# A graph network's first layer regrouped by source, and edge weights spread by a matmul

## The reference

```python
x = ln(x + segment_sum(x[src], dst))                      # first layer
x = ln(x + passes(x))                                     # ten passes
x = ln(x + convolutions(x))                               # three gated graph convolutions
x = ln(x + mean_by_dst(mlp([x[dst], x[src] - x[dst]])))   # last stage

def one_pass(f):                                          # ten times
    up = maximum(f[dst] - f[src], 0) * sqrt(w)[:, None]
    return f + maximum(segment_max(up, src), 0)
def gcn(x, W, b):                                         # with self loops and both degrees' roots
    return segment_sum(nw[:, None] * (x @ W)[src], dst) + b
```

## Time and profile before

| | |
|---|---|
| median of 3 runs | 9774.35 us (9773.21 to 9776.04) |
| the profiled execution | 9777.86 us, its span 9776.1 |
| mean granted clock of PE | 0.922 |
| busy: PE, DVE, ACT, POOL | 7043.3, 7381.2, 4251.3, 3651.6 us |
| DMA | 1233.58 MB, mean 126 GB/s |
| first matmul of the passes | 2521.5 us |
| one pass | 440 us, of which 58 steps take 401 |
| one convolution layer | 554.6 us |

### The profile page before, as it was taken

The page is one execution under the profiler, slowest core; times in us unless marked ns, Lnnn a source line. Parts: engine busy times, 40 slices in busy tenths (PEclk is TensorE's granted clock), DMA queues, the critical chain, the costliest instruction groups (busy, mean ns, idle before and its releaser), DMA issues. The chain is left out here.

```text
span 9776.1 us, 146679 instructions
## 1 busy us (share of the span) xinstructions
PE 7043.3 (72%) x44075; PEld 3621.5 (37%) x44075; DVE 7381.2 (76%) x11812; ACT 4251.3 (43%) x4937; POOL 3651.6 (37%) x3081
## 2 busy tenths in 40 slices
PE   3101299990688797979788797979698988946665
PEld 2101255550333343434343343434354555523332
DVE  8877788872687787878787787878798998954443
ACT  0000066660455454545455454545354545523333
POOL 0047788882233332423333332424100000057775
PEclk9999999995899999999999999999799999977777
DMA  2000011115776676767676676767311112111111
GB/s 83 3 11 5 6 37 42 39 37 194 241 234 216 203 243 206 242 206 241 205 233 213 206 245 206 242 204 245 90 61 51 61 46 65 63 16 27 27 27 26
DMA packets 593297, 1233.58 MB, mean 126 GB/s; under 512 B 128487, under 2 KB 241975, under 8 KB 592418
## 3 DMA queue, kind: packets, MB, share of 16 engines
q1 hardware_dynamic: 263170, 851.76, 27.2%
q10 hardware_dynamic: 231360, 335.60, 9.4%
q0 software_dynamic: 97984, 36.11, 3.1%
HBM read 992.41 MB, written 231.17 MB: 125 GB/s over the span
## 5 line engine op out<-in xcount | busy, mean ns | idle before, releaser
L1449 PE MATMUL acc<-dst_hot,parts 128*128 128x512 bf16 x11600 | 2983.3, 382 | 904.5 <-issue 665.2
L1508 ACT ACTIVATE parts_out<-acc 96x1024 bf16<-96x1024 f32 x2320 | 2314.2, 1018 | 2273.7 <-PE acc L1460 1764.0
L1413 POOL DMA_INDIRECT group_best<-best_dram,best_row x1250 | 1469.5, 1176 | 3148.4 <-SPq L1379 2773.4
L1338 DVE TENSOR_SCALAR dst_hot<-dst_rows,node_f 128x2048 bf16<-128x2048 int16 x2910 | 2047.3, 738 | 172.9 <-PE acc L1460 141.1
L1449 PEld LDWEIGHTS acc<-dst_hot,parts 128*128 x11600 | 1047.3, 97 | 2202.6 <-issue 945.5
L907 POOL DMA_INDIRECT gathered<-table_dram,gather_index x830 | 961.1, 1158 | 1967.2 <-POOLq L156 1706.8
L298 POOL DMA_INDIRECT got_src<-edges_dram,gather_index x928 | 1165.4, 1256 | 849.9 <-DVEq L746 558.8
L1460 PE MATMUL acc<-source,parts 128*128 128x128 bf16 x9280 | 909.4, 221 | 3.4 <-issue 0.3
L1006 PE MATMUL acc<-hot_space,parts 128*96 128x512 bf16 x3828 | 857.8, 380 | 42.7 <-DVE hot_space L931 42.5
L1826 DVE TENSOR_SCALAR dst_hots<-node_row,dst_col 128x640 bf16<-128x640 int16 x2436 | 827.4, 382 | 54.7
L1531 DVE SCALAR_TENSOR_TENSOR risen<-rise,factor 128x512 f32<-128x512 f32 x580 | 400.9, 691 | 606.9 <-DMA joined<-slot_inside_dram 459.6
(11 more groups left out here) (369 smaller groups left out, 7999.6 us busy)
## 6 DMA issues: line engine op xcount, KB each, us to landing
dst_rows<-step_dst_dram SPq DMA_DIRECT2D x582, 512.0 KB, 4.5
source<-source_dram SPq DMA_DIRECT2D x582, 512.0 KB, 7.8
best_dram<-best_out ACTq DMA_DIRECT2D x580, 256.0 KB
factor<-slot_weight_dram ACTq DMA_DIRECT2D x560, 256.0 KB
sources<-source_dram SPq DMA_DIRECT2D x174, 512.0 KB, 3.3
joined<-slot_inside_dram ACTq DMA_DIRECT2D x560, 64.0 KB
dst_rows<-step_src_dram SPq DMA_DIRECT2D x58, 512.0 KB, 5.9
source_dram<-source SPq DMA_DIRECT2D x58, 512.0 KB, 6.8
```

The lines of the kernel that those rows point to most:

```text
L1338: nc.vector.tensor_scalar(hot[k % 2][b][:, :], index_rows[k % 3][:, :], node_f[:, b:b + 1], None, ALU.is_equal).then_inc(hot_ready, 1)
L1413: pool.indirect_dma_start(group_best[:, g, h, :], None, best_dram, bass.IndirectOffsetOnAxis(ap=best_row[:, i:i + 1], axis=0)).then_inc(en ...
L1449: nc.tensor.matmul(acc[n % 3][:, 0:TILE], blocks[b], hot[k % 2][b][:, q * TILE:(q + 1) * TILE], start=(b == 0), stop=(b == DST_BLOCKS - 1))
L1508: act.activation(moved[n % (2 * QUADS)][:, :], acc[n % 3][0:SPLIT, :], ACT.Copy).then_inc(tile_moved, 1)
```

## The change

The first layer works on the slots by source: 58 steps as in a convolution layer, 16 source finds and 16 adds on PE with one-hots of 640 columns (all 16 by DVE), sums of all nodes in PSUM. DVE makes the source one-hots of each step in the same loop and SP stores them. The records of 20 steps (320 gathers) are fetched in the preparation, by an index turned to columns from the sorted keys with 16 transposes on PE, and the other 608 in this layer, each into its own column of `got`. After the loop the sums are closed, copied, transposed and added (25 matmuls), normalised and split; dst and root of the weight are turned to rows, the root split in three bfloat16 parts, and both stored by step. The old first layer and the separate source stage go, with the DRAM copies of dst, root and weight.

In the passes `joined` is resident, loaded once in the prologue (128 x 58 x 512 bytes). The weights come as 12 rows of 512 (three DMAs of four rows on SP's queue, after the source load and before the index load of a step); PE multiplies them with a 96 x 128 matrix `spread` after quad 1, before sum_up, and ACT copies the result to `factor` after quad 2's move. There are two PSUM pairs `acc` in place of three.

In the convolutions dst and weight columns are resident, so their preparation only normalises and stores the root; the two casts are made by ACT at quads 2 and 3, the last subtraction moves to stage 7, and PE's address arithmetic stands between the adds. In the last stage `inside` is built after hot_columns(0).

```diff
-RECORDS_FIRST = 400
+STEPS_FIRST = 20
+
+def gather_records(pool, k, got_in):
+
+    for n in range(k * STEP_SUBS, (k + 1) * STEP_SUBS):
+        pool.indirect_dma_start(got[:, n, :], None, edges_dram,
+                                bass.IndirectOffsetOnAxis(ap=record_index[:, n:n + 1], axis=0)).then_inc(got_in, 16)
...
+            for q in range(QUADS):
+                sp.dma_start(key_rows[:, q, :], sorted_dram[0, q * STEPS1 * TILE:(q + 1) * STEPS1 * TILE].rearrange("(k s) -> k s", k=STEPS1)).then_inc(key_rows_in, 16)
...
+                dve.wait_ge(key_cols_moved, 2)
+                link(V.tensor_scalar(record_index[:, :], col_key[:, :].bitcast(U32), ID_MASK, None, ALU.bitwise_and))
                 V.drain().then_inc(edge_ready, 1)
+                key_of(col_key[:, :], col_key[:, :])
+                group_of(group_base[:, :], col_key[:, :])
+                link(V.tensor_scalar(group_base[:, :], group_base[:, :], float(DST_NODES), None, ALU.mult))
+                dve.wait_ge(keys_in0, 16 * (4 + QUADS - 1))
...
-            link(V.memset(inside[1][:, :, :, 0:1], 0))
-            link(V.tensor_scalar(tmp[:, :], starts[1][:, :], -1.0, 1.0, ALU.mult, ALU.add))
-            for k in range(CHUNKS):
-                link(V.tensor_copy(inside[1][:, k, :, 1:CT + 1], tmp[:, k * CT:(k + 1) * CT].unsqueeze(1).broadcast_to([P, D, CT])))
...
+        def _(pool):
+            pool.iota(node_row[:, :], [[1, DST_NODES]], base=0, channel_multiplier=0).then_inc(const_done, 1)
+            for k in range(STEPS_FIRST, STEPS1):
+                if k >= STEPS_FIRST + 4:
+                    pool.wait_ge(got_in[k % 4], records_of(k - 4))
+                gather_records(pool, k, got_in[k % 4])
+            for k in range(STEPS1 - 4, STEPS1):
+                pool.wait_ge(got_in[k % 4], records_of(k))
...
+            for k in range(STEPS1 + 1):
+                if k < STEPS1:
+                    if k >= 2:
+                        sp.wait_ge(source_ready, k - 1)
+                    sp.dma_start(index_rows[k % 2][:, :], step_row(step_src_dram, k)).then_inc(src_in[k % 2], 16)
+                if k:
+                    c = k - 1
+                    sp.wait_ge(source_ready, c + 1)
+                    sp.dma_start(source_dram[c], source[c % 3][:, :]).then_inc(made_out[c % 3], 16)
...
+
+            def columns_of(some):
+                link(V.scalar_tensor_tensor(dst_col[:, some], got[:, some, 0], 1.0, group_base[:, some], ALU.mult, ALU.subtract))
+            columns_of(slice(0, STEPS_FIRST * STEP_SUBS))
+            for k in range(STEPS1 + 1):
+                if k < STEPS1:
+                    dve.wait_ge(src_in[k % 2], 16 * (k // 2 + 1))
+                    if k >= 3:
+                        dve.wait_ge(made_out[k % 3], 16 * (k // 3))
+                        dve.wait_ge(tile_found, (k - 2) * QUADS)
+                    V.tensor_scalar(source[k % 3][:, :], index_rows[k % 2][:, :], node_f[:, 0:1], None, ALU.is_equal).then_inc(source_ready, 1)
+                c = k - 1
+                if c >= STEPS_FIRST:
+                    dve.wait_ge(got_in[c % 4], records_of(c))
+                    columns_of(slice(c * STEP_SUBS, (c + 1) * STEP_SUBS))
+                for n in range(c * STEP_SUBS, (c + 1) * STEP_SUBS) if c >= 0 else ():
+                    if n >= HOTS1:
+                        dve.wait_ge(added, n - HOTS1 + 1)
+                    V.tensor_scalar(dst_hot[n % HOTS1][:, :], node_row[:, :], dst_col[:, n:n + 1], None, ALU.is_equal).then_inc(hot_ready, 1)
...
+            turn_columns(dst_col).then_inc(dst_turned, 1)
+            for h in range(HI):
+                b, at = divmod(h, BANK // D)
+                last = nc.tensor.matmul(sums[:, b * BANK + at * D:b * BANK + (at + 1) * D], flat_first[:, h * P:(h + 1) * P], sum_f[:, :], start=True, stop=True)
+            last.then_inc(rows_done, 1)
+            turn_columns(root_col).then_inc(weight_turned, 1)
...
+            for g in range(DST_GROUPS):
+                V.tensor_copy(flat_first[:, g * DST_NODES:g * DST_NODES + BANK], sums[0:SPLIT, g * BANK:(g + 1) * BANK])
+            V.drain().then_inc(flat_ready, 1)
+            dve.wait_ge(root_done, 1)
+            link(V.tensor_tensor(root_col[:, :], root_col[:, :], is_real[:, :], ALU.mult))
+            V.drain().then_inc(weight_ready, 1)
+            dve.wait_ge(rows_moved, 1)
+            layer_norm(dve, link, norm_ready, norm_root, 1, state[:, :, :], ends[:, :, :])
+            link(V.tensor_copy(rows[:, :, :], state[:, :, :]))
+            split_rows(link, rows[:, :, :])
+            dve.wait_ge(weight_moved, 1)
+            for i in range(3):
+                link(V.tensor_copy(root_parts[:, i, :], root_rows[:, :]))
+                if i < 2:
+                    link(V.tensor_tensor(root_rows[:, :], root_rows[:, :], root_parts[:, i, :], ALU.subtract))
+            V.drain().then_inc(weight_split, 1)
...
     def load_factor(sp, k, factor_in):
-        sp.dma_start(factor[k % 3][:, :], quads_of(slot_weight_dram, k).unsqueeze(1).broadcast_to([QUADS, D, TILE])).then_inc(factor_in[k % 3], 16)
-        sp.dma_start(joined[k % 3][:, :], quads_of(slot_inside_dram, k).unsqueeze(1).broadcast_to([QUADS, D, TILE])).then_inc(factor_in[k % 3], 16)
+        for i in range(3):
+            sp.dma_start(weight_rows[k % 3][i * D:i * D + QUADS, :], step_weight_dram[k, i]).then_inc(factor_in[k % 3], 16)
...
+            for q in range(QUADS):
+                of_quad = slot_inside_dram[q * STEPS1 * TILE:(q + 1) * STEPS1 * TILE]
+                sp.dma_start(joined[q * D:(q + 1) * D, :, :].rearrange("p k s -> p (k s)"), of_quad.partition_broadcast(D)).then_inc(joined_in, 16)
...
+                    if AHEAD <= k + 1 < STEPS1:
+                        if k >= 2:
+                            sp.wait_ge(factor_done, k - 1)
+                        load_factor(sp, k + 1, factor_in)
...
-                    if n >= 3:
-                        pe.wait_ge(tile_moved, n - 2)
+                    if n >= ACCS:
+                        pe.wait_ge(tile_moved, n - ACCS + 1)
...
+                def spread_weights(k):
+                    if k >= AHEAD:
+                        pe.wait_ge(factor_in[k % 3], 48 * loads_before(k))
+                    if k >= 2:
+                        pe.wait_ge(factor_moved, k - 1)
+                    nc.tensor.matmul(factor_sum[k % 2][:, :], spread[:, :], weight_rows[k % 3][:, :], start=True, stop=True).then_inc(factor_done, 1)
...
-                        if q == 1 and k:
-                            sum_up(k - 1)
+                        if q == 1:
+                            spread_weights(k)
+                            if k:
+                                sum_up(k - 1)
...
-                    if q == 2 and 2 <= k + 1 < STEPS1:
-                        if k >= 2:
-                            act.wait_ge(best_ready, k - 1)
-                        load_factor(act, k + 1, factor_in)
                     if q == 3 and k >= 2:
                         store_best(k - 2)
                     act.wait_ge(tile_done, n + 1)
                     if n >= 2 * QUADS:
                         act.wait_ge(sum_done, n // QUADS - 1)
-                    act.activation(moved[n % (2 * QUADS)][:, :], acc[n % 3][0:SPLIT, :], ACT.Copy).then_inc(tile_moved, 1)
+                    act.activation(moved[n % (2 * QUADS)][:, :], acc[n % ACCS][0:SPLIT, :], ACT.Copy).then_inc(tile_moved, 1)
+                    if q == 2:
+                        if k >= 2:
+                            act.wait_ge(risen_ready, k - 1)
+                        act.wait_ge(factor_done, k + 1)
+                        act.activation(factor[k % 2][:, :], factor_sum[k % 2][:, :], ACT.Copy).then_inc(factor_moved, 1)
...
-                    if c >= AHEAD:
-                        dve.wait_ge(factor_in[c % 3], 32 * loads_before(c))
-                    V.scalar_tensor_tensor(risen[:, :], rise[c % 2][:, :], 0.0, factor[c % 3][:, :], ALU.max, ALU.mult).then_inc(risen_ready, 1)
+                    dve.wait_ge(factor_moved, c + 1)
+                    V.scalar_tensor_tensor(risen[:, :], rise[c % 2][:, :], 0.0, factor[c % 2][:, :], ALU.max, ALU.mult).then_inc(risen_ready, 1)
...
+                def cast(c, i):
+                    if not 0 <= c < STEPS1:
+                        return
+                    act.wait_ge(weighed_ready, 2 * c + i + 1)
+                    if not i and c >= 2:
+                        act.wait_ge(added, (c - 1) * STEP_SUBS)
+                    act.activation(message[c % 2][:, :, i * D:(i + 1) * D], weighed[c % 2][:, :, :], ACT.Copy).then_inc(part_ready, 1)
...
+                    if q == 2:
+                        cast(k - 1, 0)
+                    if q == 3:
+                        cast(k - 1, 1)
...
-                        of_step = w_col[:, :].rearrange("p (q k j) -> p k q j", q=QUADS, j=SUBS)[:, k, :, :]
```

(20 more changed lines are left out.)

694 lines of the change are left out of this document (302 added, 392 removed).

## The result

The changed kernel takes 9131.35 us (median of 4 runs, 9127.90 to 9131.58) beside 9775.19 before on the same chip: a ratio of 0.934, with a 95% interval of 0.9324 to 0.9356. That is 644 us less. The forecast was 925 less, 8850, with a range up to 9110: the sign was right, the time lies 21 us outside the range.

The account below looks back on a forecast made before the run. It took POOL to bound the new first layer, ACT's issues and `joined` waits to slow the passes, DVE the convolutions. Terms -500 - 273 - 11 - 145 + 4 = -925 gave 8853, less 3.5: about 8850 us; range 8660 to 9110.

Parts of the forecast that it names:

- A: Start to the first matmul of the passes: POOL bounds the new first layer, source stage gone; -500 us.
- The third rival: New first layer: one-hots on DVE hold POOL, gathers at 1.61 us as in the old; 9050 us, chance 0.12.
- B: The passes: a step goes from 6.92 to 6.45 us over 580 steps; -273 us.
- So q1 starts perhaps 0.1 late: Passes: with two pairs PE waits for the tile before, at q1, adding 0.1 us a step.
- The tenth put on the store's issue: Passes: the issue of the store of best on ACT's queue at q3 adds 0.1 us a step.
- The first rival: Passes gain nothing: two pairs, copy and store on ACT take back the queue's gain; period 6.92, 9120 us, chance 0.14.
- The prediction's own sign for the passes: Passes: the prediction is wrong if a step takes over 6.9 us.
- C: Before the convolutions: DVE's wait for w_by_subtile goes, root_row is next late; -11 us of at most 17.6.
- E: Last stage: bound by POOL, whose gathers are slowed by the casts of `inside` now built there; +4 us.
- D: Convolution steps: two casts of 0.42 us leave DVE, a step goes from 8.67 to 7.83; -145 us.
- 2 to 3 us: Convolution steps: time until DVE asks for a cast queued on ACT, two or three of eight stages later.
- The second rival: Convolutions gain nothing: the chain DVE, ACT, DVE, ACT, DVE takes the casts' time; 8995 us, chance 0.10.

Follow-up runs that it names:

- e17: e9 with the records of 24 steps instead of 20 fetched in the preparation, on a quick chip: 8693.06 us, ratio to before 0.8888.
- e9: Changed kernel with three PSUM pairs for acc (one bank each for rise and factor_sum) and ACT's second convolution one-hot after the last quad: 8759.65 us.
- e10: Changed kernel, two pairs, address computation of the passes left out (every tile uses the first tile's addresses): 8802.55 us, ratio to before 0.9003.
- e11: Kernel before with joined loaded only once, in the prologue, not in each step: 9393.30 us, ratio to before 0.9609.
- e12: Kernel before with factor loaded only once, in the prologue, not in each step: 9406.15 us, ratio to before 0.9621.
- e8: Kernel before with factor and joined issued on SP's queue instead of ACT's: 9780.10 us, ratio to before 1.0005.
- e18: e9 with two more 64 KB loads a step on SP's queue (128 rows of 512 bytes each), on a quick chip: 8770.30 us, ratio to before 0.8967.
- e3: Changed kernel with ACT's second convolution one-hot made after the last quad, on a slower chip: 10113.36 us, ratio to before 0.9784.
- e2: Changed kernel with the next tile's addresses computed behind the five gather matmuls, on a slower chip: 10385.05 us, ratio to before 1.0047.
- e6: Changed kernel with the addresses for the tile after the first quad's computed at the end of the fourth quad: 9139.33 us, ratio to before 0.9350.
- e14: e9 with the records of 24 steps instead of 20 fetched in the preparation, on a slower chip: 9726.78 us, ratio to before 0.9435.

## Why the prediction was right and wrong

**A was right**, in mechanism and size: POOL bounds the new first layer (e17), a gather at 1.278 us for 1.28, 488 us of 500. The third rival, POOL held by the one-hots, did not come: with DVE busy 140.4 of 150 us, 126.4 of it in 640-wide one-hots, the gather took 1003 ns and 0.30, 0.06 over its price beside an idle DVE. "SBUF — State Buffer" ("Who interferes with whom") in the Trainium skill has the other engine fully blocked for the whole of a DVE instruction in a 2-port mode. No trace here shows the mode, but the traces show that the cost goes with the length of the instruction: 0.36 us a gather beside one-hots of 0.75 us, 0.06 beside those of 0.3.

**B was wrong, in two terms of its sum.** The step failed that says "So q1 starts perhaps 0.1 late", which is the whole price of the two pairs. It followed one quad, q1 (the second of a step), and asked only when the engine would get its pair. PE gets that pair in time (2249.96 for 2250.48). The cost came one quad earlier, in q0, the first of a step, for which the sum had no wait: its pair too is free in time for the engine (2248.56 for 2248.64), but too late for the sequencer, which passes the wait only then and has the address work still before it. The trace has this quad 0.49 longer, three pairs give back 0.42 a step (e9), and without address work two pairs are harmless (e10). The second term is the weights' matmul, 0.31 for 0.25. Of the forecast 6.45 the sum's 5.99 + 0.25 + 0.1 + 0.1 becomes 5.99 + 0.31 + 0.49 less 0.09 in the second quad, 6.70; the mean over the passes is 6.78. The tenth put on the store's issue did not come.

The forecast gain of 0.47 a step was there: e9 has 6.36, 0.54 under the mean of 6.90 before. More than three quarters of it, 0.42, the changed kernel lost again for want of the third pair. The reading of the kernel before was half right: the transfers held it, since removing either small one frees it (e11, e12). That ACT's queue was the cause was wrong: with the issues on SP the time stays (e8), and the long issues go over to SP's queue. Nor was it the bytes alone, as 257 GB/s in e11 shows, or the packets alone, as 122 per us in e18 do. What the threshold is stays open; for this mix of transfers it lies between the load of before and that load less 64 KB a step.

The first rival was priced at 9120, 11 us from what came, and that is chance: it had nothing from the passes and 145 us from the convolutions, where 70 and 78 came. Its mechanism is only partly what happened: two pairs took back most of the gain, while the copy and the store on ACT took none that shows (with three pairs both remain in e9). The prediction's own sign for the passes, a step over 6.9, did not come either: it was 6.78, so that sign was too coarse for this miss.

**C and E were right**: 13 for 11, and +3 for +4.

**D was wrong in one term.** "A cast queues behind a found move or the one-hots of ACT, and DVE asks for it two or three of eight stages later, 2 to 3 us" had the mechanism, and the failed term is its "2 to 3 us": DVE asked for the first cast 0.9 us after its message was ready, and the cast only began 1.0 us after it. The wait is 0.64 to 0.74 a step. With the one-hot moved (e9) the step is 7.51, better than the forecast 7.83. The rows of DVE account for it: the two casts took 0.90 from their starts to those of the next instructions, and the multiplication and the first subtraction, which no longer make DVE wait for their own end, now have the next instruction 0.60 and 0.61 behind their start, for 0.72 and 0.72 before. This was not tried by itself.

The range ended 21 us short. The second rival lay in it, and the first just beyond its end, but three quarters of the first together with half of the second had no place in it.

## What to carry to other kernels

A buffer ring is slack for the sequencer as well as for the engine: before taking one buffer away, find the instructions behind its wait that issue nothing to the engine (register loads, address arithmetic), for they are hidden only as long as the sequencer can run ahead. Where a change frees one resource, price the next bound without its slack: here 0.54 us a step was freed, and 0.42 of it lost for want of a third PSUM pair that one bank each of two other rings would have paid for. And when work moves to a second engine in the middle of a chain, write out that engine's queue in order at that moment; one reordering was worth 126 to 128 us (e3, e9).

## What the runs showed that was not expected

- Computing the same addresses elsewhere in the tile (e2) or a tile earlier (e6) gained nothing or cost 150 us; leaving them out gained 329 us (e10). The work is five register operations of 115 ns a tile and a load:

```profile
L1415 PEldq FUSED_REGOPS  x11590: 52/115/218, 2032.2 to 6323.4; - x200
```

- On two of the chips the same kernels took 5 to 13% longer: before 10298 to 10332 for 9775, e14 9727 for the 8693 of e17, at waits of several us that the trace calls "remote" or "issue". The relative gain of an edit differs there (0.9435 against 0.8888), so an edit must be judged on one chip.
- The loads of before held the passes at 239 GB/s and 108 packets per us, while e11 ran free at 257 GB/s and e18 at 122 packets per us. In the held versions the issues themselves are long, on ACT's queue up to 4.6 us before and on SP's 3.6 in the median in e8; in e12 none of joined's issues takes over 0.53.
